# Two fused low-rank-adapted linear layers: short weight-times-factor passes placed between the long passes of the matrix merge

## What is computed

```python
# x: (8, 256, 1024) float32; both index vectors: 8 integers
x = x + (x @ W0.T + b0 + 2 * (x @ A0[i]) @ B0[i])
x = x + (x @ W1.T + b1 + (x @ A1[j].T) @ B1[j].T)
```

## Time and profile before

| | |
|---|---|
| Median of 3 runs | 313.38 us |
| Lowest and highest | 311.9 and 313.47 us |
| The profiled execution: its own time | 312.38 us |
| The profiled execution: span in the profile | 310.8 us |
| TensorE matmuls: busy, number | 298.8 us, 1420 |
| TensorE weight loads: busy, number | 247.6 us, 1420 |
| VectorE busy | 193.7 us |
| ScalarE busy | 89.7 us |
| Granted TensorE clock, mean of the span | 1.00 |

### The profile page before, as it was taken

One profiled execution on the slowest core, in us unless ns is written; L12 is line 12 of the kernel. 1 busy time (PEld: TensorE's weight loads), 2 busy tenths in 40 slices (PEclk: granted clock), 3 DMA queues, 4 the chain that ended last, 5 costly groups with the idle time before them and its releaser, 6 DMA issues.

```text
span 310.8 us, 3985 instructions
## 1 busy us (share of the span) xinstructions
PE 298.8 (96%) x1420; PEld 247.6 (80%) x1420; DVE 193.7 (62%) x325; ACT 89.7 (29%) x142; POOL 18.5 (6%) x43
## 2 busy tenths in 40 slices
PE   0999999999999999998999999999999999999995
PEld 0888898888887488886888888888888888888884
DVE  4777624994749362188896776487486485585312
ACT  4555424112123302293224123232232322232000
POOL 2443140000000010000000000000000000000000
PEclk9999999999999999999999999999999999999999
DMA  7996140000000155504054360440641621602002
GB/s 268 382 347 226 48 159 12 0 0 2 0 0 3 17 178 209 166 0 135 0 194 138 115 184 34 152 147 34 187 141 38 211 78 70 219 35 85 18 34 101
DMA packets 14456, 33.94 MB, mean 109 GB/s; under 512 B 2117, under 2 KB 2117, under 8 KB 14438
## 3 DMA queue, kind: packets, MB, share of 16 engines
q1 hardware_dynamic: 13414, 31.60, 30.1%
q0 software_dynamic: 1024, 2.10, 2.1%
HBM read 22.09 MB, written 11.60 MB: 108 GB/s over the span
## 4 chain that ended last, share of the span: by engine, by line
PE 92%; DVE 4%; ACT 2%; DMA 1%; issue 0%; SPq 0%
PE bank L766 29%; PE bank L861 16%; PE bank L860 16%; PE bank L862 16%; PE bank L880 4%; PE bank L778 3%; PE bank L867 3%; DMA stage<-W1T 1%; PE bank L835 1%; PE bank L837 1%; PE bank L836 1%; PE bank L780 1%; DVE w L562 1%; PE bank L808 1%; PE bank L846 1%; PE bank L847 1%
## 5 line engine op out<-in xcount | busy, mean ns | idle before, releaser
L766 PE MATMUL bank<-w,w_hi 128*128 128x512 f32 x256 | 80.7, 397 | 7.0 <-ACT w L325 7.0
L766 PEld LDWEIGHTS bank<-w,w_hi 128*128 128x128 f32 x256 | 48.7, 192 | 17.9 <-ACT w L325 7.0
L766 PE MATMUL bank<-w,w_lo 128*128 128x512 f32 x128 | 50.1, 391 | 0.0
L376 ACT CAST xa<-xr 128x512 fp32r<-128x512 f32 x32 | 19.6, 621 | 33.9 <-PE bank L867 15.0
L766 PEld LDWEIGHTS bank<-w,w_lo 128*128 128x128 f32 x128 | 24.2, 189 | 5.1
L861 PE MATMUL bank<-w_lo,w 128*128 128x512 f32 x64 | 25.1, 392 | 0.0
L862 PE MATMUL bank<-w_hi,w 128*128 128x512 f32 x64 | 25.0, 391 | 0.0
L860 PE MATMUL bank<-w_hi,w 128*128 128x512 f32 x64 | 25.0, 391 | 0.0
L861 PE MATMUL bank<-w 128*128 128x512 f32 x64 | 25.0, 391 | 0.0
L860 PE MATMUL bank<-w 128*128 128x512 f32 x64 | 25.0, 391 | 0.0
L860 PE MATMUL bank<-w_hi,xa 128*128 128x512 f32 x64 | 25.0, 390 | 0.0
(11 more groups left out here) (119 smaller groups left out, 487.0 us busy)
## 6 DMA issues: line engine op xcount, KB each, us to landing
xr<-xT SPq DMA_DIRECT2D x32, 256.0 KB, 4.4
out<-stage SPq DMA_DIRECT2D x28, 256.0 KB, 2.1
stage<-W SPq DMA_DIRECT2D x8, 512.0 KB, 4.9
stage<-W1T SPq DMA_DIRECT2D x8, 512.0 KB, 6.0
a<-rb_rows SPq DMA_DIRECT2D x8, 392.0 KB
rb_rows<-a SPq DMA_DIRECT2D x3, 512.0 KB
rb_rows<-b0w SPq DMA_DIRECT2D x3, 512.0 KB
out<-rows SPq DMA_DIRECT2D x4, 256.0 KB, 2.2
```

The costliest lines, as they stand in the source:

```text
L376: nc.scalar.copy(x_op(j, 0), raw(j)).then_inc(op_hi[j], 1)
L766: return mm(d_bank(m, h)[:, :], left[:, m, k * P:(k + 1) * P], right[:, k, h * HALF:(h + 1) * HALF], start=start, stop=stop)
```

## The change

The passes of `aux(4)` to `aux(8)` no longer stand in runs of 16 between the row blocks. `d_tile` takes for each of its halves the number of an auxiliary block, or none. Within the three long passes of each k it issues the short high pass behind the first long pass and the short low pass behind the second (for the last k the low one first, as before). Block 5 carries 4 in its first half, block 2 carries 5 and 6, block 6 carries 7 and 8; blocks 3 and 7 carry none. The wait on `aux_done` stands at the head of the half. No matmul, weight load or operation of another engine is added or removed, and the operands are the same. In the queues of ScalarE and VectorE the readers of the auxiliary sums change places with readers of the blocks, and with `bias_add`, to fit the new order in which the sums end.

```diff
@@ ScalarE
-            aux_copy(4)
             high_bottom(4)
             high_top(1)
+            aux_copy(4)
             high_bottom(5)
             aux_copy(5)
+            aux_copy(6)
             high_top(2)
-            aux_copy(6)
-            high_bottom(6)
             aux_copy(7)
             aux_copy(8)
+            high_bottom(6)
@@ VectorE
-            g_add(4)
             low_bottom(4)
             low_top(1)
+            g_add(4)
             bias_add(0)
             bias_add(1)
             low_bottom(5)
             g_add(5)
             bias_add(2)
             bias_add(3)
+            g_add(6)
             low_top(2)
-            g_add(6)
             bias_add(4)
             bias_add(5)
-            low_bottom(6)
             g_add(7)
             g_add(8)
+            low_bottom(6)
             bias_add(6)
             bias_add(7)
@@ TensorE
+            def aux_high(j, k, start, stop):
+                return mm(banks[6 + j % 2][:, 0:2 * BR], w0_hi[:, AUX[j], k * P:(k + 1) * P], a1[:, k, :],
+                          start=start, stop=stop)
+
+            def aux_low(j, k):
+                return mm(banks[6 + j % 2][:, 0:BR], w0_lo[:, AUX[j], k * P:(k + 1) * P], a1[:, k, 0:BR],
+                          start=False, stop=False)
+
-            def d_tile(m):
+            def d_tile(m, js=(None, None)):
                 for h in range(NH):
+                    j = js[h]
+                    if j is not None:
+                        pe.wait_ge(aux_done, j - 1)
                     for k in range(KT):
+                        closes = k == KT - 1
                         d_pass(m, h, k, w0_hi, w1_hi, k == 0, False)
+                        if j is not None and not closes:
+                            aux_high(j, k, k == 0, False)
+                        elif j is not None:
+                            aux_low(j, k)
                         d_pass(m, h, k, w0_hi, w1_lo, False, False)
-                        last = d_pass(m, h, k, w0_lo, w1_hi, False, k == KT - 1)
+                        if j is not None and not closes:
+                            aux_low(j, k)
+                        elif j is not None:
+                            aux_high(j, k, False, True).then_inc(aux_summed, 1)
+                        last = d_pass(m, h, k, w0_lo, w1_hi, False, closes)
                 last.then_inc(d_summed, 1)
...
-            aux(4)
             pe.wait_ge(d_lo[B11], 1)
             pe.wait_ge(top_t1, 1)
-            d_tile(5)
-            aux(5)
+            d_tile(5, (4, None))
             pe.wait_ge(t4_made, 1)
-            d_tile(2)
-            aux(6)
+            d_tile(2, (5, 6))
             pe.wait_ge(d_lo[B11], 2)
             pe.wait_ge(top_t1, 2)
-            d_tile(6)
-            aux(7)
-            aux(8)
+            d_tile(6, (7, 8))
```

More of the change, by code:

```diff
@@ L767, in d_pass @@
                           right[:, k, h * HALF:(h + 1) * HALF], start=start, stop=stop)
+            def aux_high(j, k, start, stop):
[4 more added lines that the diff above has]
+                          start=False, stop=False)
             def aux(j):
-                m = AUX[j]
@@ L771, in aux @@
                 if j >= 2:
                     pe.wait_ge(aux_done, j - 1)
[L773 to L780, removed]
@@ L781, in aux @@
-                last.then_inc(aux_summed, 1)
-            def d_tile(m):
+                for k in range(KT - 1):
+                    aux_high(j, k, k == 0, False)
+                    aux_low(j, k)
+                aux_low(j, KT - 1)
+                aux_high(j, KT - 1, False, True).then_inc(aux_summed, 1)
+            def d_tile(m, js=(None, None)):
                 for h in range(NH):
+                    j = js[h]
+                    if j is not None:
+                        pe.wait_ge(aux_done, j - 1)
```

## The result

| | before | after |
|---|---|---|
| Median, us (12 runs each) | 313.13 | 313.59 |
| Profiled execution: span, us | 310.8 | 312.5 |
| TensorE matmuls: busy, us | 298.8 | 300.5 |

The ratio is 1.0027, with a 95% interval from 1.0014 to 1.0040: the kernel is slower by 0.85 us (0.4 to 1.3). The plain difference of the two medians is 0.46 us, that of the two means 0.70 us (313.65 - 312.95); both lie in that interval. I had forecast no change. The measured time lies in the range, and the loss is less than the 0.5% that I had called noticeable, but twelve runs on each side tell it from nothing.

What follows compares the result with a forecast made beforehand. TensorE's own sequence was taken to bound the kernel: 312.38 + 0.0 (steps) + 0.0 (waits) = 312.4 us for the profiled execution; the median, 1.0 us above at 313.38, was taken as 313.2, range 310.2 to 315.0.

Steps and rivals of the forecast that it cites:

- the 0.5% that I had called noticeable: Whole kernel: a measurement was said to tell about 0.5% (1.6 us) from no change.
- What bounds, and the waits: TensorE: only its own sequence or new waits count; possible new waits between st and `c` were all said to be covered.
- my 101.3: VectorE behind block 6: last `bias_add` forecast to end at 101.3, before `c` wants it at 104.7; 3.4 us cover.
- The short passes: Aux 4 to 8 on TensorE: high pass 0.118 us; low pass 0.112, all of it the load of its successor.
- rival 2: Loads behind low passes are hidden between long passes: 2.2 us gained, 311.0 us; chance 0.23.
- The long passes beside them: Three long passes per k at 0.227 us each, unchanged beside short ones; k step 0.911 us before and after.
- the mark of 0.02: Sign of being wrong: a k step with both short passes differing from 0.911 us by more than 0.02.
- rival 3: Mixing costs at each of 80 short passes, up to 0.075 us each; put at 316.2 us; chance 0.09 together with rival 4.
- rival 1: No change in the whole kernel, likeliest: 313.2 us, own range 312.0 to 314.3; chance 0.68.

Runs made afterwards that it cites:

- t_only: TensorE's part of the change alone, with ScalarE's and VectorE's orders as in the kernel before; ratio 1.0019 (1.0006 to 1.0032) to the kernel before.
- wide512_after: Changed kernel with the short passes made 512 columns wide, sums not right, executed once; five passes of a k take 1.13 us, 0.226 each.

## Why the prediction was wrong

- **What bounds, and the waits.** Right. TensorE alone counts; it met no new wait, in the changed kernel or in `t_only`. The last four operations of `bias_add`:

```profile
97.81 5.23 DVE L529 SCALAR_TENSOR_TENSOR rows<-w,b_raw,rows 128x1024 f32<-128x1024 f32 x4
```

  They end at 97.81 + 5.23 = 103.04; less 1.04 of later start and 0.7 of longer stretch that is my 101.3. `c` starts at 106.46, so `r` hides them with 3.4 us to spare, as forecast.
- **The short passes.** Right in their lengths: 0.120 and 0.108 us, where I had put 0.118 and 0.112. The long neighbours did not shorten the low pass, and rival 2 is out. That it is the next load which sets its 0.11 us fits all runs, but stays a reading.
- **The long passes beside them.** This is the term that failed. I wrote 3 x 0.227, a pace read in rows of long passes only, and took it into a sequence in which no long pass has two equal neighbours. It measured 0.232 to 0.235 in the changed kernel. The step was 0.930 instead of 0.911 us, which is 0.019 off and just inside the mark of 0.02 that I had named as the sign of being wrong: the mark was too wide for 40 steps (0.8 us).
- **The evidence I gave against it was false.** Under rival 3 I wrote that the entry and the exit of the aux runs show no such step. I had looked at the entry. The exit was in the trace of before, at the start of block 5 (matmuls):

```profile
51.65 0.63 PE L766 MATMUL bank<-w,w_hi 128*128 128x512 f32 x2
52.12 0.39 PE L766 MATMUL bank<-w,w_lo 128*128 128x512 f32 x1
```

  Two long passes take 0.47 us, 0.235 each. In the kernel before, three blocks begin behind such an exit, and the long passes behind one cost 0.02 to 0.03 us more together; the change makes 80 returns.
- **Rival 3** is what happened, with the mechanism half right: the price is not on the short pass but on the long ones near it, 0.009 us for each short pass, not up to 0.075, and neither bank nor operand matter. I had let it count only from 0.02 us a pass on, 1.6 us. A loss below that was to me "no change".
- **The range.** That 313.59 us lies in 310.2 to 315.0 says nothing for the sum: the range was made wide for rival 2 and for the spread of single runs. Its upper bound for rival 2, 311.8, is also not rival 1's 314.3 less 2.2, which is 312.1; nothing rests on it.

Open is why equal steps settle: the runs show that a step of another length, or weights at an odd place, each keep the passes from it, and how long it lasts varies from three to ten passes. What in the engine or in its reads does it was not shown.

## What to carry to other kernels

Putting short matmuls between long ones did not shorten them here: a pass of 128 columns took 0.11 us in a run of short ones and between long ones alike. Count each step as the longer of its columns and that 0.11 us, in whatever order they come. A duration taken from a uniform row is good for uniform rows; for a mixed sequence read the first passes behind a change of length too, and multiply by how many such places the change makes. Keep passes of a kind together in runs of 16 or so. Let weights begin at multiples of 256 bytes, where that is free; the 0.20 us it gave in `r` is seen in the trace alone.

## What was not expected of the hardware

Float32r passes of 512 columns run at 0.227 us in a settled row and at 0.230 to 0.235 us on the mean otherwise, at the same granted clock of 1.00. A row settled three to ten passes behind a step of another length (256 or 128 columns); with 384 columns between, the long passes took 0.232. Weights beginning 8 or 64 bytes off a multiple of 256 bytes kept it unsettled for a whole block (0.231 and 0.233 us a pass), 256 bytes off did not (0.227). Changing the PSUM bank, the moving tile and the weights at every pass cost nothing: 0.227 us in `wide512_after`.
